# A four-layer kernel: routing, the experts' last products and second matmuls and the convolution one step later, the last top-1 product ahead of the next row's projections

## The reference

```python
x = _layernorm(x + attention(x))   # per query: 64 local keys and 32 more, picked by an index score; 8 heads
x = _layernorm(x + experts(x))     # 16 experts of width 64, the best 4 per token, and one shared expert
x = _layernorm(x + scan(x))        # in-projection, 4-tap causal convolution, SiLU, state scan (16 states), gate
x = _layernorm(x + top1(x))        # 8 experts, the best one per token, with a capacity over all tokens

# experts
scores = sigmoid(x @ gate_w.T)
idx = top_k(scores + gate_b, 4);  comb = 2.5 * scores[idx] / sum(scores[idx])
y = sum_e comb_e * (silu(x @ w13_e.gate) * (x @ w13_e.up)) @ w2_e  +  the shared expert

# scan
x, z = split(h @ in_proj);  u = silu(conv4(x) + conv_b)
dt, B, C = split(u @ x_proj);  delta = softplus(dt @ dt_proj + 2 * dt_b)
state = exp(delta * A) * state + delta * B * u;  y = (sum_n state * C + u * D) * silu(z) @ out_proj
```

## Time and profile before

| what | value |
|---|---|
| median of 3 runs (lowest, highest) | 1443.02 us (1440.24, 1448.51) |
| the profiled execution's own time | 1442.37 us |
| its span | 1440.6 us |
| mean granted TensorE clock | 0.768 |
| DVE busy | 990.2 us (69%) |
| PE busy | 908.0 us (63%) |
| ACT busy | 584.6 us (41%) |
| chain that ended last, by engine | DVE 37%, PE 26%, issue 16%, ACT 13%, DMA 4%, SP 3% |

### The profile page before, as it was taken

The page is one execution under the profiler, slowest core; times in us unless marked ns, Lnnn a source line. Parts: engine busy times, 40 slices in busy tenths (PEclk is TensorE's granted clock), DMA queues, the critical chain, the costliest instruction groups (busy, mean ns, idle before and its releaser), DMA issues.

```text
span 1440.6 us, 30987 instructions
## 1 busy us (share of the span) xinstructions
PE 908.0 (63%) x11808; PEld 541.5 (38%) x11808; DVE 990.2 (69%) x2294; ACT 584.6 (41%) x1278; POOL 83.8 (6%) x56
## 2 busy tenths in 40 slices
PE   4556656778456576677656568577757567562555
PEld 2334534445224253444323335344424235240122
DVE  4355553566799986655789986746789987344985
ACT  2423332566552332376544232366643331444320
POOL 0000000010000000011000000011000000030630
PEclk9566868597769789688769779598757879575895
DMA  4110110311232210221123310031033310302320
GB/s 140 30 39 10 32 39 10 68 35 35 70 82 76 57 31 18 51 50 38 62 62 79 82 30 7 13 88 39 15 92 96 79 34 10 67 0 60 110 66 8
DMA packets 84840, 72.38 MB, mean 50 GB/s; under 512 B 24528, under 2 KB 63440, under 8 KB 84496
## 3 DMA queue, kind: packets, MB, share of 16 engines
q1 hardware_dynamic: 84688, 70.34, 19.2%
HBM read 66.51 MB, written 3.80 MB: 49 GB/s over the span
## 4 chain that ended last, share of the span: by engine, by line
DVE 37%; PE 26%; issue 16%; ACT 13%; DMA 4%; SPq 3%; DVEq 1%; ACTq 0%; POOL 0%; POOLq 0%
DVE SG L1725 5%; PE bank L708 4%; PE bank L536 3%; DVE Y L1818 3%; PE bank L740 3%; SPq L473 2%; DVE XP L1738 2%; ACT relu_s L1016 2%; DVE CV L1738 2%; PE bank L866 2%; DVE bank L1725 1%; ACT QBD L1052 1%; DVE ml L1460 1%; PE bank L816 1%; DVE big L1700 1%
## 5 line engine op out<-in xcount | busy, mean ns | idle before, releaser
L708 PE MATMUL bank<-onehot,tparts 128*32 128x256 bf16 x3840 | 134.9, 300 | 46.0 <-DVE onehot L1499 45.1
L708 PEld LDWEIGHTS bank<-onehot,tparts 128*32 128x32 bf16 x3840 | 107.2, 105 | 82.6 <-DVE onehot L1499 44.4
L866 PE MATMUL bank<-XP,CO 128*128 128x512 f32 x128 | 84.6, 796 | 63.4 <-DVE XP L1736 33.8
L1725 DVE TENSOR_TENSOR_SCAN SG<-big 128x512 f32<-128x512 f32 x96 | 111.8, 1206 | 5.3 <-DVE score L1429 1.8
L1201 ACT ACTIVATE big<-DEL,Aneg 128x512 f32<-128x512 f32 x96 | 63.8, 715 | 109.1 <-DVE SG L1725 103.1
L1016 ACT ACTIVATE relu_s<-bank,nml 128x192 f32<-128x192 f32 (+1 forms) x128 | 53.0, 426 | 113.2 <-DVE nml L1465 113.2
L866 PE MATMUL bank<-CV,CO 128*128 128x512 f32 x128 | 74.1, 707 | 38.4 <-DVE CV L1738 26.3
L1499 DVE TENSOR_SCALAR onehot<-ib,CO 128x1024 bf16<-128x1024 f16 x160 | 69.8, 478 | 16.2 <-PE bank L708 11.0
L740 PE MATMUL bank<-GT,QBD 128*32 128x32 f32 x3072 | 55.8, 206 | 39.1 <-DVE G L1508 27.9
L1460 DVE TENSOR_REDUCE ml<-bank 128x2 f32<-128x384 f32 (+1 forms) x64 | 33.8, 569 | 67.1 <-PE bank L643 36.5
L536 PE MATMUL bank<-CO,relu_s 128*128 128x128 f32 (+2 forms) x256 | 46.2, 341 | 47.8 <-ACT relu_s L1016 47.8
(11 more groups left out here) (313 smaller groups left out, 1999.4 us busy)
## 6 DMA issues: line engine op xcount, KB each, us to landing
BC<-bc_rows SPq DMA_DIRECT2D x128, 256.0 KB, 4.4
ib<-idx_rows SPq DMA_DIRECT2D x64, 256.0 KB, 4.1
big<-comb_rows SPq DMA_DIRECT2D x8, 1024.0 KB, 10.1
rows_bounce<-RO SPq DMA_DIRECT2D x256, 8.5 KB
W<-w SPq DMA_DIRECT2D x1, 2818.0 KB, 15.1
RB<-rows_bounce SPq DMA_DIRECT2D x16, 136.0 KB, 2.1
X<-x SPq DMA_DIRECT2D x4, 256.0 KB, 3.0
out<-CV SPq DMA_DIRECT2D x4, 256.0 KB, 2.3
```

Of the source, the lines that this page charges most:

```text
L708: m = mm(bank[2 + c % 2][32 * bb:32 * bb + 32, 256 * kind:256 * kind + 256], tparts[:, kt, part, 32 * kind:32 * kind + 32], onehot[:, n % ...
L866: mm(bank[5 + j][:, :], ident, hC[(n - 1) % 2][:, j, :], start=(n == 1), stop=(n == DS)).then_inc(ysum.sem, ysum.up())
L1725: m = dve.tensor_tensor_scan(state, decay, dBu[:, n % 2, j, :], 0.0, ALU.mult, ALU.add)
```

## The change

Phases are moved as follows.

- Routing on DVE goes from r = 1 to r = 2, together with the first gate-by-up product. The transpose of `comb` on PE goes from r = 2 to r = 3, behind the matmuls of k = 1; ACT's copy goes to r = 3 behind the clamp of k = 1; SP's store and spread go to r = 3.
- `hidden(k)` goes from r = 2k + 3 to 2k + 4, behind the gate-by-up product of k + 1. `second(k)` goes from r = 2k + 4 to 2k + 6; `second(7)` and `second(8)` are both at r = 19.
- The sigmoid is computed in place in one half of `SG`, so that two halves turn (`SG_of`). A second buffer for the hidden product is `DU[:, 0]`, which is not in use there (`HT_of`). Waits follow: the clamp of k waits for `hidden(k - 2)`, `hidden(k)` for `second(k - 2)`. When alone, three of each turn as before, also in place.
- The convolution's halves are at r = 23 and 24, u's sigmoids at r = 24 and 25, the products by z's sigmoid at r = 25 with the first of u's, the second at r = 26. Everything from `u @ x_proj` to the read-out's end stands one phase later on all engines. Step 47 is added to `TWICE`, so that from there on phases stand in the same steps as before.
- `top1_out(3)` comes directly behind `top1_out(2)`, in front of the next row's projections; PE waits only for `e_used` 5 between them.

No instruction with data is added or taken away. The diff, cut:

```diff
-        req = SG[:, 1, 0:NT * NE * TOP_E]...
+        req = SZ[:, 0, 0:NT * NE * TOP_E]...
+        def ring(alone):
+            return 3 if alone else 2
+        def SG_of(k, alone):
+            return SG_turn[k % 3][:, 0, :] if alone else SG[:, k % 2, :]
+        def HT_of(k, alone):
+            return HT_turn[k % 3] if alone else (HT[:, :], DU[:, 0, :])[k % 2]
...
 # PE, rest
                     mm(bank[k0 + 1][0:rows, :], wu, XRT[:, :], start=True, stop=True).then_inc(up_ps.sem, up_ps.up())
-                    yield
-                    if k == 0:
+                    if k == 1:
                         pe.wait_ge(comb_ok.sem, comb_ok.at(b, 1))
...
-                    if k >= lag:
-                        second(k - lag)
-                    yield
-                for k in range(9 - lag, 9):
+                    if k >= 2:
+                        second(k - 2)
+                    yield
+                for k in (7, 8):
                     second(k)
...
-                for _ in range(3):
+                for _ in range(4):
                     yield
                 pe.wait_ge(u_ok.sem, u_ok.at(b, 2))
...
                 top1_out(2)
-                pe.wait_ge(e_used.sem, e_used.at(b, 4))
-                pe.sem_inc(hold_pe, 1)
-                yield
                 pe.wait_ge(e_used.sem, e_used.at(b, 5))
                 pe.sem_inc(hold_pe, 1)
                 top1_out(3)
-                yield
-                yield
-                yield
+                for _ in range(4):
+                    yield
 # ACT, rest
-                    if k >= T:
-                        act.wait_ge(sg_ok.sem, sg_ok.at(b, k - T + 1))
-                    clamped(bank[k0][0:rows, :], SGk[0:rows, 0, :], gm_ok)
+                    if k >= R:
+                        act.wait_ge(hu_ok.sem, hu_ok.at(b, k - R + 1))
+                    clamped(bank[k0][0:rows, :], SGk, gm_ok)
...
-                    yield
-                    act.wait_ge(gm_ok.sem, gm_ok.at(b, k + 1))
-                    sigmoid_logs(SGk[0:rows, 0, :])
-                    if k == 0:
-                        act.wait_ge(comb_ok.sem, comb_ok.at(b, 1))
-                    if k >= T:
-                        act.wait_ge(hu_ok.sem, hu_ok.at(b, k - T + 1))
-                    A(SGk[0:rows, 1, :], SGk[0:rows, 0, :], ACT.Exp, scale=-1.0).then_inc(sg_ok.sem, sg_ok.up())
-                    if k == 0:
+                    if k == 1:
                         act.wait_ge(ct_ps.sem, ct_ps.at(b, 1))
                         A(CT[:, :], bank[7][0:NE, :], ACT.Copy).then_inc(ct_sb.sem, ct_sb.up())
+                    yield
+                    act.wait_ge(gm_ok.sem, gm_ok.at(b, k + 1))
+                    sigmoid_logs(SGk)
+                    A(SGk, SGk, ACT.Exp, scale=-1.0).then_inc(sg_ok.sem, sg_ok.up())
                     yield
...
 # DVE, rest
+                yield
                 dve.wait_ge(rest_done.sem, rest_done.at(b, 0))
...
                 for k in range(9):
-                    if k >= lag:
-                        hidden(k - lag)
                     if k >= 1:
                         yield
...
-                    yield
-                for k in range(9 - lag, 9):
-                    hidden(k)
+                    if k >= 1:
+                        hidden(k - 1)
+                    yield
+                hidden(8)
...
-ROUTE_PHASES, EXPERT_PHASES, NORM_PHASES, SCAN_IN_PHASES, SCAN_OUT_PHASES, TOP1_PHASES = 2, 18, 2, 10, 3, 8
-TWICE = (33, 39, 56)
+ROUTE_PHASES, EXPERT_PHASES, NORM_PHASES, SCAN_IN_PHASES, SCAN_OUT_PHASES, TOP1_PHASES = 3, 17, 2, 11, 3, 8
+TWICE = (33, 39, 47, 56)
```

More of the change, by code:

```diff
@@ L795, in rest @@
                 yield
-                T, lag = turns(alone), 1 + alone
+                T, R = turns(alone), ring(alone)
                 def second(k):
@@ L804, in second @@
                     for i in range(NT):
[L805 removed]
+                        m = mm(bank[7][:, i * P:(i + 1) * P], HT_of(k, alone)[0:kk, i * P:(i + 1) * P], wt,
                                start=(k == 0 and i == 0), stop=(k == 8), skip_group_check=True)
@@ L1275, in rest @@
                 pool.wait_ge(rest_done.sem, rest_done.at(b, 0))
-                for _ in range(ROUTE_PHASES + 2):
+                for _ in range(ROUTE_PHASES + 1):
                     yield
@@ L1284, in rest @@
                     yield
-                for _ in range(EXPERT_PHASES - 18 + NORM_PHASES + SCAN_IN_PHASES):
+                for _ in range(EXPERT_PHASES - 17 + NORM_PHASES + SCAN_IN_PHASES):
                     yield
@@ L1632, in hidden @@
                         dve.wait_ge(ga_used.sem, ga_used.at(b, 1))
-                    if k >= T:
-                        dve.wait_ge(y_part.sem, y_part.at(b, k - T + 1))
-                    TT(HT_turn[k % T][0:rows, :], SG_turn[k % T][0:rows, 1, :], GU_turn[k % 3][0:rows, :],
+                    if k >= R:
+                        dve.wait_ge(y_part.sem, y_part.at(b, k - R + 1))
+                    TT(HT_of(k, alone)[0:rows, :], SG_of(k, alone)[0:rows, :], GU_turn[k % 3][0:rows, :],
                        ALU.mult).then_inc(hu_ok.sem, hu_ok.up())
```

16 lines of the change are left out of this document (7 added, 9 removed).

## The result

The changed kernel is slower. Over four runs each on one chip its median is 1458.85 us, that of the kernel before 1444.46; the ratio is 1.0128, 95% interval 1.0097 to 1.0159, so about 18 us. The forecast was 1447.4 (+5.0), with a range of 1430 to 1457; the measured time lies above it. A small loss was forecast, and the loss is nearly four times as large.

What follows compares the result with a forecast made beforehand. No engine was full overall; DVE, busiest at 69%, idled waiting for ACT's sigmoid and POOL's product but was full in the scan. From 1442.4, -0.9 + 1.5 + 5.4 - 3.2 + 2.2 = +5.0 gave 1447.4 us, range 1430 to 1457.

Steps and rivals of the forecast that it cites:

- Term 1: Experts beside tile 0, three woven rows: late comb mostly absorbed, last chunk's turn slightly earlier; -0.3 us a row, -0.9 in all.
- 5.0 us for an expert against the 4.8 of before: Tile 0's chain of gate matmul, clamp, copy, product, one-hot and pick would take 5.0 us per expert with `hidden` inside.
- only 0.7 us between them: Tile 0: picking would end 0.7 us before ACT's row copying the first picked latents, so PE's 1.8 us lateness costs nothing.
- Term 2: Experts' end, three rows: `second(7)` and `second(8)` together delay DVE's sum and what follows by about 0.5 us each; +1.5.
- Term 3: Convolution to read-out, three rows: standing one step later replaces DVE's waits with longer ones; +5.4 us in all.
- about 1 in small ones: Small DVE waits, steps 25 to 32, counted within the 7.5 us idle before, against 9.3 forecast after.
- the last state fills 1.7 us: Read-out's end: last state fills 1.7 us of waiting at a local maximum, DVE waits 1.2 more for PSUM's sum; net 0.
- Term 4: Top-1 output ahead of projections, two row ends: DVE's 3.71 us wait goes, projections start later; -1.6 a row, -3.2.
- Term 5: Last row alone: k = 1's matmuls stand before comb's transpose, making it 2.2 us later with nothing to hide it; +2.2.
- The bubbles go: Rival: experts' waits for ACT, 21 us over three rows, disappear because POOL and comb are early enough; 1427 us, chance 0.2.
- The clock falls: Rival: behind `hidden(1)` PE drops to 1.2 GHz, pick and gate matmul double over two experts; 11 us, 1458, chance 0.15.
- The shift is hidden: Rival: moves at experts and convolution only replace waits; just the top-1 move and the last row count; 1441.4, chance 0.15.

Runs made afterwards that it cites:

- b_exp_front: Experts' part alone on the kernel before, but comb's transpose and copy, still in the late step, ahead of k = 1's matmuls and clamp: 1443.72 us, ratio 1.0003.
- b_exp_pool: Experts' part alone on the kernel before, plus POOL's product waiting until DVE's `hidden` is done: 1443.45 us, ratio 0.9999.
- c_shift: Kernel before with everything from `u @ x_proj` to the read-out's end one step later, convolution whole in its old step: 1453.81 us, ratio 1.0062.
- b_top: Kernel before with only the last top-1 product moved ahead of the next row's projections: 1439.98 us, ratio 0.9982.
- b_conv: Kernel before with only the convolution's split and everything behind it one step later, step 47 taken twice: 1447.24 us, ratio 1.0035.
- c_split: Kernel before with the convolution's second half, z's sigmoid products and u's second sigmoid one step later, the rest unshifted: 1439.61 us, ratio 0.9977.
- c_em: Kernel before with the shift from `u @ x_proj` on, convolution whole, softplus's last two ACT passes behind the attention's weights: 1447.99 us, ratio 1.0052.
- after_mend: Changed kernel with comb in its old steps, POOL waiting for `hidden`, softplus's last two passes later: 1444.21 us, ratio 1.0012 to the kernel before.
- best_ets: Kernel before with later `hidden` and `second`, two buffers, comb in old steps, top-1 move, and convolution split without shift: 1439.54 us, ratio 0.9962.
- best_etp: Kernel before with later `hidden` and `second`, two buffers, comb in old steps, top-1 move, POOL waiting for `hidden`: 1434.82 us, ratio 0.9949.
- b_exp: Kernel before with only the experts' part: routing and comb later, `hidden` and `second` later, two buffers: 1453.29 us, ratio 1.0068.

## Why the prediction was right or wrong

Measured apart, the experts' part is +9.8 (forecast +2.8), the convolution's +5.1 (+5.4) and the top-1 move -2.6 (-3.2). That is +12.3; the whole is +18.5.

**Term 1, experts beside tile 0 (-0.9): wrong, the main failure.** By the account of stages it is, together with term 2, +8.8 in the changed kernel. On comb's way each time up to `hidden(1)` was right within a microsecond. What failed is the step "the chain ... with `hidden` now inside it: 5.0 us for an expert against the 4.8 of before". It was 6.1 us (the gate-by-up products of k = 3 and 4 at 301.73 and 307.83). Durations were taken from rows in which POOL and DVE did not meet and PE was at 2.4 GHz. In the new order `hidden(1)` costs 1.74, a one-hot 1.50, the first pick 1.47. The sign of it stood in the earlier trace rows: in the last row `hidden` took 1.66 us, where POOL's second product begins beside it, and was not read. And "only 0.7 us between them" of slack was read as safety; b_exp_front and b_exp_pool show that there was none to spare: the experts' part alone is +9.8, and +0.4 with comb 1.4 us earlier. A second reading failed too: ACT's copy of the first picked latents, forecast at 296.5, came at 298.15 behind its own sigmoid. The local scores did not bring ACT forward; its spread of the queries started 0.7 us later than before, not 1 us earlier. The last chunk's turn was 4.0 us behind its forecast.

**Term 2, the experts' end (+1.5)**: not separated. DVE waits 4.0 us in four places for the second matmuls at the experts' sum, 3.5 in three before.

**Term 3, convolution (+5.4)**: alone +5.1, so the size was right, but by luck, by cancelling: the shift is +9 and the split -3 (with 0 in the interval). The term's own sum also slipped: its 7.5 us of before hold "about 1 in small ones", its 9.3 of now do not. Counted alike the first row is +2.8 and not +1.8. The forecast waits came as written: 3.24 for the queries, 0 for RB, 2.52 for `em`, 2.41 at the local maximum. The step that failed is the one behind them, "the last state fills 1.7 us ... 1.2 us more for the sum in PSUM: 0": the wait at the read-out did rise by 3.9 us over the run (4.6 to 8.5), and the piece from the last state on is 1.5 to 2.0 us shorter a row in c_shift, but the stretch of the states, at which the sum put nothing, is 2.6 longer a row. Together with the experts' part it costs 7 to 10.6 us more than the two alone, which a sum of terms could not have; the cause of that is open.

**Term 4, top-1 (-3.2): right, as far as can be told.** The stage is 3.4 us shorter in the change's profile, and the forecast wait of the norm for ACT's scale is there (1.66 us). The projections start 3.0 us later against the top-1 layer's first sum, where 3.2 was forecast (the term's own 1.6 and 1.9 make 3.5). Alone the move is -2.6 with 0 in its interval, and in b_top's own profile the stage is only 1.1 shorter.

**Term 5, the last row alone (+2.2): wrong, it is 0.4.** The matmuls of k = 1 did stand in front, but the second of them ran at the higher level of the clock. So they ended 1.1 us after DVE's routing (which ended at 1262.0), not 2.3 us, and the transpose took 0.60 us, not 1.01:

```profile
1260.39 2.03 PE L826 MATMUL bank<-XRT,W 128*128 128x512 f32 x2
...
1262.26 1.02 PE L827 MATMUL bank<-XRT,W 128*128 128x512 f32 x2
...
1263.12 0.60 PE L546 MATMUL bank<-CO,HT 128*16 128x128 f32 x4
```

"From 1242.3 to 1246.1" had them at 1.2 GHz throughout. POOL came 0.4 us later than before, counted from the routing's end (16.9 us behind it instead of 16.5). That the clock was high here is not shown to be the move's doing: of the kernels without those matmuls in front six (b_conv, c_split, c_shift, c_em, after_mend, best_ets) have 0.60 us in the last row too, and ten have 1.01.

**The rivals.** "The bubbles go" fell: the waits moved to the instruction ahead of `hidden`. "The clock falls" named the right place, and its time, 1458, was met; its row is there (0.86 for 0.98, pick 1.47), as the Trainium skill (TensorE: Matmul & The Clock Gate, "HAM oscillation") would have it of an engine that waits for a transfer each time. But its mechanism was at most a small part. In the changed kernel only the first pick and half of the first gate matmul ran slow, the next ones took 0.84 and 1.13 us, where the rival had both slow over two experts; and PE was at the lower level already before its 2.12 us of idle time there (its index scores at 291.81 took 1.01 us, 0.59 before). b_exp_front has the low clock and costs nothing that can be told. The time was met by luck, by a sum of other causes. "The shift is hidden" fell with c_shift.

## What to carry to other kernels

When an instruction is moved next to another engine's work, take its duration from rows where they stand side by side, not from rows where they don't; and where an estimate leaves less than a microsecond between two chains, treat the outcome as open, since on this kernel 1.4 to 1.9 us more of lateness in a row went with 8 us over three rows. A part that comes out near its forecast may be two parts that cancel: run them apart. A move that relies on a DMA's result should keep the DMA's start where it was; best_etp keeps comb early, moves only its users, and gains most. And when an added wait takes a collision away, look where the delayed instruction now runs: POOL's product met another one-hot, at a place where a wait covered it in part.

## What the runs showed of the hardware

- Of POOL and DVE, which got in each other's way, the one that started first kept its time, and the other was late. `hidden` begun 0.07 to 0.15 us behind POOL's product took 1.66 to 1.74 us instead of 0.69, and POOL's its usual 1.27; begun 0.16 to 0.26 us ahead of it, `hidden` took 0.68 to 0.69 and POOL's product 1.55 to 1.66. A one-hot (`tensor_scalar`, bf16) begun 0.25 us ahead of POOL took 0.47 us, begun behind it up to 1.51. One more wait on POOL took away the slow `hidden`, but left three slow one-hots.
- The Trainium skill (SBUF — State Buffer, "Who interferes with whom") says that a DVE instruction with two SBUF inputs contends with a GpSimd instruction that reads SBUF. It says further that a `tensor_scalar` can enter a mode with two ports, in which the engine that issues first holds the shared ports for the whole instruction and the other is blocked. The trace agrees on the order, by the times above; whether this one-hot ran in that mode no row shows. The gate-by-up product, with one input in PSUM, ran beside a POOL product only in the last row of four kernels (0.43 us at 1253.79 in best_etp, for one), and both took their usual 0.68 and 1.27 us.
- In b_exp PE's first product after a wait of 5.09 us ran for the most part at the lower level of the clock (1.47 for 0.84 us); the matmuls ahead of the wait had run at the higher level (0.60 us for the index scores at 291.18). In the changed kernel it took the same 1.47 us, but there PE was at the lower level before the wait.
